# Products of 128x128 weights as two of 64 columns beside each other, and all transposes in 64-row halves: three shapes of TensorE's array in place of four

## The reference, cut to what matters

```
# part A, B=8, S=512, D=128: 16 query heads of 64, 8 key/value heads
q = einsum('bsd,dhe->bshe', x, W_Q);  k, v = x @ W_K, x @ W_V
p = softmax(mask_causal(q . k / 8));  z = p @ v
x = norm(x + einsum('bshe,ehd->bsd', z, W_out) + b_out)
# part B, twice: 8 heads of 64, windows of 64 tokens that see one window back
h = shift_token(x)                    # the upper 64 columns come from the token before
q, k, v = split(h @ wqkv)             # 128 -> 3 * 512
q, k = rotary_xpos(l2norm(q) * qs, l2norm(k) * ksc)
x = x + local_attention(q, k, v) @ wo # 512 -> 128
h = layernorm(shift_token(x)) * lg + lb
a, g = split(h @ w1 + b1)             # 128 -> 2 * 341
x = x + (a * gelu(g)) @ w2 + b2       # 341 -> 128
# and at the end x = norm(x)
```

## Time and profile before

| | us |
|---|---|
| median of three runs | 1186.05 |
| the profiled execution, its own time | 1185.78 |
| its span in the profile | 1183.9 |
| TensorE busy with matmuls | 1163.0 |
| VectorE, ScalarE, GpSimd busy | 1040.4, 1004.0, 965.3 |
| MATMUL instructions | 14280 |

### The profile page before, as it was taken

The page is one execution under the profiler, slowest core; times in us unless marked ns, Lnnn a source line. Parts: engine busy times, 40 slices in busy tenths (PEclk is TensorE's granted clock), DMA queues, the critical chain, the costliest instruction groups (busy, mean ns, idle before and its releaser), DMA issues.

```text
span 1183.9 us, 38698 instructions
## 1 busy us (share of the span) xinstructions
PE 1163.0 (98%) x14280; PEld 857.0 (72%) x14280; DVE 1040.4 (88%) x3947; ACT 1004.0 (85%) x3078; POOL 965.3 (82%) x957
## 2 busy tenths in 40 slices
PE   9999999999999999999999999999999999999987
PEld 7677676777677776777777777777777877677665
DVE  7888988898998989999899989989899898988874
ACT  7787988889888988899888898888988889887785
POOL 3777887888789797897878987899878988798963
PEclk9999999999999999999999999999999999999999
DMA  6001001001011010100001100011101101010100
GB/s 224 19 12 25 20 22 22 18 21 23 20 27 27 13 31 20 23 21 22 22 20 23 25 18 22 21 23 26 27 4 26 27 21 23 11 27 23 26 18 18
DMA packets 31067, 31.34 MB, mean 26 GB/s; under 512 B 12576, under 2 KB 21408, under 8 KB 30752
## 3 DMA queue, kind: packets, MB, share of 16 engines
q1 hardware_dynamic: 30448, 28.08, 9.7%
q10 hardware_dynamic: 432, 0.79, 0.2%
HBM read 9.98 MB, written 2.10 MB: 10 GB/s over the span
## 4 chain that ended last, share of the span: by engine, by line
PE 90%; DVE 5%; ACT 4%; issue 1%; DMA 1%; POOL 0%; POOLq 0%; SPq 0%; DVEq 0%; ACTq 0%
PE psum L644 12%; PE psum L680 12%; PE psum L657 7%; PE psum L810 6%; PE psum L794 5%; PE psum L787 5%; PE psum L756 5%; PE psum L619 5%; PE psum L689 5%; PE psum L720 5%; PE psum L715 4%; PE psum L725 4%; PE psum L818 3%; PE psum L771 3%; PE psum L738 3%; PE psum L627 2%
## 5 line engine op out<-in xcount | busy, mean ns | idle before, releaser
L857 ACT ACTIVATE prob<-prob,negmax 128x512 f32<-128x512 f32 (+3 forms) x512 | 284.3, 558 | 11.4 <-DVE negmax L1005 10.1
L1005 DVE CUSTOM_DVE_ANT_0 prob<-psum,causal 128x512 f32<-128x512 f32 (+3 forms) x512 | 232.1, 481 | 3.5 <-PE psum L644 2.0
L1208 POOL TENSOR_SCALAR prob<-prob,rowinv 128x384 f32<-128x384 f32 (+1 forms) x256 | 160.8, 642 | 76.8 <-DVE rowinv L1011 76.6
L912 ACT ACTIVATE b_prob<-b_prob,b_negmax 128x128 f32<-128x128 f32 x512 | 198.9, 396 | 3.9 <-DVE b_negmax L1086 3.9
L1228 POOL TENSOR_TENSOR r<-r 128x512 f32<-128x512 f32 x128 | 162.6, 1274 | 37.4 <-DVE r L1044 37.2
L644 PE MATMUL psum<-k_t,q_t 64*128 64x384 f32 (+3 forms) x1024 | 178.4, 451 | 2.2 <-ACT qk_t L904 1.1
L680 PE MATMUL psum<-prob_t,v 128*64 128x256 f32 x1280 | 151.4, 381 | 0.0
L1086 DVE CUSTOM_DVE_ANT_0 b_prob<-psum,band,rnorm 128x128 f32<-128x128 f32 x512 | 146.4, 345 | 3.4 <-PE psum L756 2.1
L1211 POOL TENSOR_TENSOR prob<-prob,rowinv 128x512 f32<-128x512 f32 x96 | 98.0, 1042 | 45.8 <-DVE rowinv L1011 45.8
L657 PEld LDWEIGHTS psum<-ident,prob 64*128 64x128 f32 x2560 | 98.7, 138 | 34.7 <-issue 25.9
L864 ACT COPY prob_t<-psum 128x512 f32<-128x512 f32 (+1 forms) x176 | 95.6, 544 | 32.8 <-PE psum L657 32.6
(11 more groups left out here) (107 smaller groups left out, 2880.7 us busy)
## 6 DMA issues: line engine op xcount, KB each, us to landing
vb_mid<-vb SPq DMA_DIRECT2D x112, 128.0 KB, 2.3
x_t<-in_x_t SPq DMA_DIRECT2D x8, 256.0 KB, 3.0
x_n<-in_x SPq DMA_DIRECT2D x8, 256.0 KB, 2.8
x<-x SPq DMA_DIRECT2D x64, 31.8 KB
out<-x SPq DMA_DIRECT2D x15, 128.0 KB, 2.2
wqkv<-in_wqkv SPq DMA_DIRECT2D x1, 1536.0 KB, 11.5
x<-x SPq DMA_DIRECT2D x48, 0.2 KB
w<-in_w SPq DMA_DIRECT2D x1, 682.0 KB, 13.4
```

Of the source, the lines that this page charges most:

```text
L857: last = af(pr, pr, ACT.Exp, bias=negmax[:, k % 4, o:o + 1], scale=-1.0, accum_out=rowsum[:, k % 4, o:o + 1])
L912: last = af(pr, pr, ACT.Exp, bias=b_negmax[:, a, o:o + 1], scale=-1.0, accum_out=b_rowsum[:, a, o:o + 1])
L1005: vec.tensor_tensor_reduce(prob[:, k % PROBS, h, p * K:(p + 1) * K], bank[:, p * K:(p + 1) * K], causal[:, S - K:S], -E ** -0.5, 3.0e38, A ...
L1208: last = gp.tensor_scalar(pr, pr, rowinv[:, k % 4, h:h + 1], 1.0, ALU.mult, ALU.mult)
```

## The change

Every product with 128 columns of weights is issued as two, `halves`: columns 0 to 63 into PSUM partitions 0 to 63, columns 64 to 127 into partitions 64 to 127, of the same bank, with the same moving rows. The transposes of `b_h` and `b_turn_f` are issued as two of 64 rows, each into a bank of its own, and are copied out in two instructions for each engine. `w1` is padded from 341 to 384 columns, so that its last block has 128 columns instead of 85. The planner loses the full shape and gets other numbers in its tables; `LATE`, `BY_ACT` (4 to 3) and `BY_DVE` (0 to 8) change too.

```
-BANKS, LATE = 8, 16
-SINGLES, BY_ACT, BY_DVE = 2, 4, 0
+BANKS, LATE = 8, 15
+SINGLES, BY_ACT, BY_DVE = 2, 3, 8
-SWITCH, TABLES, SHY, PULL = {"128x128": 202, "64x128": 155, "128x64": 150, "64x64": 97}, 1283, 110, 0.01755
+SWITCH, TABLES, SHY, PULL = {"64x128": 155, "128x64": 150, "64x64": 97}, 1283, 380, 0.04162
...
-MARGIN = 0, 50
+MARGIN = 200, 150
-FULL, HALF, COLS, QUARTER = "128x128", "64x128", "128x64", "64x64"
+HALF, TURN, COLS, QUARTER = "64x128", "64x128t", "128x64", "64x64"
+AFTER_TURN = 55
+def entry_ns(shape, entered):
+    if shape.rstrip("t") != entered.rstrip("t"):
+        return SWITCH[entered.rstrip("t")]
+    return AFTER_TURN if shape == TURN and entered == HALF else 0
...
-        step("pe", "b_h", k, 109, [source, ("pe", "b_v", ahead)], FULL, [[("act", "b_h", k), ("dve", "b_h", k)]])
+        step("pe", "b_h", k, 66, [source, ("pe", "b_v", ahead)], TURN, [[("act", "b_h", k), ("dve", "b_h", k)]] * 2)
...
+            def halves(out, weights, moving, start=True, stop=True):
+                for w in range(2):
+                    last = mm(out[half(w)], weights[:, half(w)], moving, start=start, stop=stop)
+                return last
...
                 for c in range(4):
-                    last = mm(bank[:, c * P:(c + 1) * P], wq[:, 4 * h + c, :], x_t[:, b % 2, i * P:(i + 1) * P], start=True, stop=True)
+                    last = halves(bank[:, c * P:(c + 1) * P], wq[:, 4 * h + c, :], x_t[:, b % 2, i * P:(i + 1) * P])
...
-                bank, = claim("b_h", l, n)
-                transpose(bank[:, 0:P], src, ident[:]).then_inc(h_done, 1)
+                banks = claim("b_h", l, n)
+                for q in range(2):
+                    last = transpose(banks[q][:, 0:E], src[half(q), :], ident[half(q), half(q)])
+                last.then_inc(h_done, 1)
...
-                bank, = banks_of("b_h", l, n)
-                copy(h_t[0:E, l, t * P:(t + 1) * P], bank[0:E, 0:P]).then_inc(h_act, 1)
+                for q, bank in enumerate(banks_of("b_h", l, n)):
+                    last = copy(h_t[0:E, l, t * P + q * E:t * P + q * E + E], bank[0:E, 0:E])
+                last.then_inc(h_act, 1)
```

More of the change, by code:

```diff
@@ L626, in project_k @@
                 for c in range(GA // 2):
-                    last = mm(bank[:, c * P:(c + 1) * P], wk[:, c, :], x_t[:, b % 2, i * P:(i + 1) * P], start=True, stop=True)
+                    last = halves(bank[:, c * P:(c + 1) * P], wk[:, c, :], x_t[:, b % 2, i * P:(i + 1) * P])
                 last.then_inc(k_done, 1)
@@ L688, in out_a @@
                 for c in range(CA):
-                    last = mm(bank[:, 0:D], z_t[:, (NT * b + i) % 2, c, :], wout[:, c, :], start=(c == 0), stop=(c == CA - 1))
+                    last = halves(bank[:, 0:D], z_t[:, (NT * b + i) % 2, c, :], wout[:, c, :], start=(c == 0), stop=(c == CA - 1))
                 last.then_inc(out_done, 1)
@@ L793, in wo_b @@
                 for c in range(CB):
-                    last = mm(bank[:, 0:D], o_t[:, c, :], wo[:, l, c, :], start=(c == 0), stop=(c == CB - 1))
+                    last = halves(bank[:, 0:D], o_t[:, c, :], wo[:, l, c, :], start=(c == 0), stop=(c == CB - 1))
                 last.then_inc(wo_done, 1)
@@ L798, in turn_f @@
                 pe.wait_ge(x_hat_ready, nth("pool", "b_norm", (l, g)))
-                bank, = claim("b_turn_f", l, g)
+                banks = claim("b_turn_f", l, g)
                 for k in range(SIZE[g]):
-                    last = transpose(bank[:, k * P:(k + 1) * P], x_hat[:, k, :], ident[:])
+                    for q in range(2):
+                        last = transpose(banks[q][:, k * E:(k + 1) * E], x_hat[half(q), k, :], ident[half(q), half(q)])
                 last.then_inc(f_turned, 1)
             def ffn(l, g, ch):
-                k, z = MCH[ch], SIZE[g] * P
+                z = SIZE[g] * P
                 pe.wait_ge(f_ready, nth("act", "b_turn_f", (l, g)))
@@ L808, in ffn @@
                 for part in (1, 0):
-                    o = part * HID + ch * P
-                    last = mm(bank[0:k, (1 - part) * z:(2 - part) * z], w1[:, l, o:o + k], f_t[:, 0:z], start=True, stop=True)
+                    last = halves(bank[:, (1 - part) * z:(2 - part) * z], w1[:, l, part, ch * P:(ch + 1) * P], f_t[:, 0:z])
                 last.then_inc(ffn_done, 1)
@@ L939, in turn_f @@
                 act.wait_ge(ffn_done, nth("pe", "b_ffn", (*group_before(l, g, 1), CH - 1)))
-                bank, = banks_of("b_turn_f", l, g)
-                z = SIZE[g] * P
-                af(f_t[:, 0:z], bank[:, 0:z], ACT.Identity, scale=ln_gb[:, l, 0:1], bias=ln_gb[:, l, 1:2]).then_inc(f_ready, 1)
+                z = SIZE[g]
+                f_rows = f_t[:, 0:z * P].rearrange("p (k q n) -> p q k n", k=z, q=2)
+                for q, bank in enumerate(banks_of("b_turn_f", l, g)):
+                    last = af(f_rows[:, q, :, :], bank[:, 0:z * E].rearrange("p (k n) -> p k n", k=z), ACT.Identity, scale=ln_gb[:, l, 0:1], bias=ln_gb[:, l, 1:2])
+                last.then_inc(f_ready, 1)
             def gelu(l, g, ch):
```

101 lines of the change are left out of this document (51 added, 50 removed), and 3 rows, old and new, of the table HURRY.

## The result

The changed kernel takes 1178.93 us, the median of four runs (1178.41 to 1179.63), against 1185.95 for the kernel before on the same chip: a ratio of 0.994 (0.9928 to 0.9953). It is faster by 7.0 us. The forecast was 17.8 and 1168: the direction is right, but only four tenths of the forecast gain are there. The question is where the rest went.

The account below looks back on a forecast made before the run. The prediction took TensorE's own steps to bound the kernel. Its terms, -16.3 + 0 - 6.1 + 5.6 - 1 = -17.8 us, took 1185.8 to 1168.0, with an 8-in-10 range of 1156 to 1183.

Parts of the forecast that it names:

- What bounds the kernel: Whole kernel: TensorE's own steps set the time, being 98% busy and 90% of the chain of waits.
- The entries, -16.3 us: TensorE's changes into a step shape from another, priced at 0.15 to 0.20 us each: fewer of them save 16.3 us.
- The pairs, 0, low end -4: Full products issued as two 64-column halves: same cost as before, 0, at best 4 us saved.
- instructions that aren't hidden: Rival: 3124 added MATMULs with their weight loads cost 0.029 us each, unhidden, +91 us, 1259; chance 6%.
- The transposes, -6.1: 128 transposes of L702 and L801 on TensorE, issued in halves, get 0.05 us cheaper each: -6.1 us.
- The warm products, +5.6 and -1: Warm products go from 46 to 71 pairs: +5.6 us of TensorE's time, 1 given back for waits they fill.
- What the other engines get, 0 in the sum: Doubled copies and moved work on ScalarE and VectorE are hidden by idle time: 0, up to +15 us in the range.
- The waits, counted as unchanged: TensorE's waits for other engines: no term of their own in the sum, apart from 1 us given back for warm products.
- The work is saved but other engines are late: Rival: a third to half of ScalarE's and VectorE's added work becomes TensorE waits, +8 to +15, about 1180; chance 20%.
- More than the sum: Rival: the planner's 200 ns more per hand-over removes a third of waits, and pairs save 4: about 1158; chance 20%.
- The entries aren't gone: Rival: the 0.15 to 0.20 us belongs to changing kind of step, not shape, so no change, 1186; chance 3%.
- The clock: Rival: TensorE falls to its lower clock level for want of full-size products, everything slower; chance 1%.

Follow-up runs that it names:

- full_arrays: The changed kernel, orders, banks and copies untouched, with each product issued as one full 128x128 product again: 1217.85 us, ratio 1.027.
- few_warm: The changed kernel with 46 warm pairs in the tail, as many as before, in place of 71: 1178.6 us, ratio 0.9941.
- one_copy: The changed kernel without the second copies of b_h on ScalarE and VectorE and of b_turn_f on ScalarE (computation incomplete): 1174.36 us, ratio 0.9904.
- before_split: The kernel before, own order and shapes, with only the copies of b_h and b_turn_f issued in two halves: 1191.56 us, ratio 1.0048.
- after_moved: The changed kernel with steps moved a few places within each engine's order; steps, banks, shapes and copies stay: 1168.79 us, ratio 0.9853.
- before_moved: The kernel before with steps moved within its orders by the same search for the same time: 1182.51 us, ratio 0.9972.
- light_after: The changed kernel, same orders, with ScalarE and VectorE copying only half the columns of part A's turned probabilities (computation incomplete): 1175.71 us, ratio 0.9914.

## Why the prediction was wrong, step by step

- *What bounds the kernel.* Right for before. For after it assumed that the chain would stay TensorE's; it fell from 90% to 78%. "Waits of TensorE in the dense part well over 5 us", one of its own signs of being wrong, came: 12.6.
- *The entries, -16.3 us.* Right in mechanism and price: 1.88 against 1.73 and 1.05 against 0.86 are in the chain of full_arrays. Only the full shape's 0.20 is 0.15 where a transpose enters it. Over the kernel full_arrays paid 39 us of the 47 that all prices make, so a part of such a sum falls into waits.
- *The pairs, 0, low end -4.* They bring 0.005 us on each of 1158 products on 128 rows, about 6 us, a little more than the low end; on 512 rows 0.86 stays 0.86. The rival of instructions that aren't hidden is refuted: 3124 more MATMULs cost nothing.
- *The transposes, -6.1.* Right: the chain after has L721 x2 at 0.06, and at 0.21 with its entry of 0.15.
- *The warm products, +5.6 and -1.* Wrong by all of it: few_warm shows 0.3 at most. That error and the pairs' would have made the gain larger than forecast.
- *What the other engines get, 0 in the sum.* This is the step that failed. It said that their idle time hides the doubled copies, since TensorE's waits on them were short, and it took all other waits over unchanged from before. The added work wasn't the trouble: ScalarE got to 1010.3 us busy and VectorE to 1047.6, below the 1022 and 1056 that it forecast. The copies cost 4.6 us (one_copy) to 5.6 (before_split). ScalarE and VectorE had the idle time; it didn't lie where the copies are, since TensorE reads the copies or refills those banks next. Idle shares of 12 and 15% say nothing of that.
- *The waits, counted as unchanged.* The second half of the failure. Entries, transposes and pairs bring 28 us by the measured prices; 7.0 came. Of the missing 21 the copies are some 5. Moving steps within the orders gives back 10.1, but 3.5 could be had before as well, so that at equal care 13.7 of the 28 came. Of the other 14 the copies are again some 5, and some 3 are entries, of which moving made 16 more here and 5 fewer in the kernel before. Some 6 us are left: after_moved still has 9.5 us without a matmul in the dense part, before_moved, by the same count, 5.9, and a part of the prices may not be paid in full, as in full_arrays. Whether a better order would get these too, or the hand-over times between tiles forbid it, stays open. So does what the second bank costs that each of these transposes now holds: before_split doubled the copies alone, and no run the banks.
- *The rivals.* "The work is saved but other engines are late" had the right place, at 20%, but the wrong mechanism: it put the lateness down to how full the engines are, and light_after shows that 30 us less for each leaves the waits. "More than the sum" expected the planner's 200 ns of margin to remove waits; there were 17 more of them. "The entries aren't gone" and "The clock" are out: 0.86 and 0.87 behind the values, and a granted clock of 1.00.

## What to carry to other kernels

When a saving comes with a new static order, its price list tells what TensorE's steps cost and not how long it waits: put a term for the new order's waits into the sum, and measure an order's worth by itself (here 46 us between two tables of numbers, 10 us by moving steps a few places). Even with fewer waits than before, after_moved got 17 of the 28 us. Work that is added to an engine with idle time is free only if nobody waits for that very result or bank: look at what TensorE does next with them rather than at the busy share. And compare two kernels of this kind at orders of equal care: 1182.5 and 1168.8 say what the shapes are worth, 1186 and 1179 do not.

## What the runs showed of the hardware that was not expected

- A wait of TensorE of 0.27 us cost 0.49: the step behind it took 1.14 us in place of 0.92. Behind a wait of 0.43 us the transposes took 0.71 in place of 0.51.
- Two halves of 64 columns side by side are slightly quicker than the full product on 128 rows of data, 1.75 us against 1.78 to 1.79 for eight, in spite of twice the instructions; on 512 rows both take 0.86.
- Entering the 128x128 shape cost 0.20 us for products and 0.15 for a transpose (L707 0.26 behind another shape, 0.11 in a run).
- One ScalarE copy that reads 64 columns from each of two neighbouring banks took 257 ns, as much as one of 128 columns from a single bank (254); two copies of 64 columns one behind the other took 0.31 us together, not twice their 0.206.
